# Counting a group of landed gather tiles three groups behind instead of two

## What is computed

```python
# N = 12501 nodes, D = 128, 150000 edges, LAYERS = 2
h = emb; acc = emb
for _ in range(LAYERS):
    h = segment_sum(adj_val[:, None] * h[adj_col], adj_row, num_segments=N)
    acc = acc + h
graph_item_embs = acc / (LAYERS + 1)
combined = graph_item_embs[items] + item_features[items]
...                                   # session attention, sess_emb [512, 128]
scores = (W_K * l2norm(sess_emb)) @ l2norm(graph_item_embs).T
```

## Time and profile before

| | |
|---|---|
| median of 3 runs | 4200.8 us (4196.42 to 4205.08) |
| profiled execution, its own time | 4204.8 us |
| its span, first to last instruction | 4203.0 us |
| busy: VectorE, GpSimd, TensorE, ScalarE | 3060.5, 2796.8, 2735.4, 810.9 us |
| mean granted TensorE clock | 0.771 |
| DMA moved | 231.36 MB, mean 55 GB/s |

### The profile page before, as it was taken

The page is one execution under the profiler, slowest core; times in us unless marked ns, Lnnn a source line. Parts: engine busy times, 40 slices in busy tenths (PEclk is TensorE's granted clock), DMA queues, the critical chain, the costliest instruction groups (busy, mean ns, idle before and its releaser), DMA issues.

```text
span 4203.0 us, 81683 instructions
## 1 busy us (share of the span) xinstructions
PE 2735.4 (65%) x14549; PEld 2365.5 (56%) x14550; DVE 3060.5 (73%) x7307; ACT 810.9 (19%) x2729; POOL 2796.8 (67%) x2868
## 2 busy tenths in 40 slices
PE   4999997555655566565664656565565655655798
PEld 2777776555555565555554555555555555553454
DVE  8999998867766677666665666676676766667575
ACT  0999997000000000000000000000000000004553
POOL 2477766767777777667775767677777777775770
PEclk8898898777777667777766766777777778786899
DMA  1000000222222222222225222222222222243143
GB/s 35 3 4 3 3 3 3 59 50 52 53 52 53 53 52 54 50 51 53 52 54 159 55 48 52 52 55 52 53 53 53 52 52 54 53 112 102 53 154 147
DMA packets 153059, 231.36 MB, mean 55 GB/s; under 512 B 65760, under 2 KB 106104, under 8 KB 152504
## 3 DMA queue, kind: packets, MB, share of 16 engines
q0 software_dynamic: 89760, 164.71, 16.9%
q1 hardware_dynamic: 48076, 59.06, 4.4%
q10 hardware_dynamic: 14796, 3.77, 0.7%
HBM read 186.08 MB, written 41.29 MB: 54 GB/s over the span
## 4 chain that ended last, share of the span: by engine, by line
POOL 28%; DMA 24%; issue 22%; PE 9%; DVE 9%; ACTq 4%; ACT 3%; SPq 0%; DVEq 0%; POOLq 0%
POOL ring L627 26%; DMA ring<-in_L_rec_emb,ring 12%; DMA ring<-table,ring 10%; ACTq L742 3%; PE bank L1598 2%; PE bank L1657 2%; ACT big L701 2%; DVE stage L976 1%; POOL ring L654 1%; DVE big L920 1%; PE bank L1685 1%; DVE big L936 1%; PE bank L1644 1%; POOL sorted_edges L587 1%; PE bank L1626 1%
## 5 line engine op out<-in xcount | busy, mean ns | idle before, releaser
L1598 PE MATMUL bank<-ring,shared 128*128 x9952 | 1809.1, 360 | 1248.2 <-POOLq L616 949.2
L1598 PEld LDWEIGHTS bank<-ring,shared 128*128 128x128 f32 x9952 | 1701.0, 268 | 1356.3 <-issue 1355.6
L1290 DVE TENSOR_TENSOR acc<-acc,bank 128x256 f32 x2488 | 1032.7, 415 | 945.0 <-PE bank L1598 936.8
L627 POOL DMA_INDIRECT ring<-table,ring x1146 | 1083.1, 945 | 462.4 <-issue 316.7
L627 POOL DMA_INDIRECT ring<-in_L_rec_emb,ring x1146 | 1089.0, 950 | 448.7 <-issue 318.5
L1240 DVE TENSOR_SCALAR shared<-bank,mlo,mval 128x256 f32<-128x256 f32 x2488 | 1334.9, 537 | 0.0
L717 ACT COPY mlo<-ring 128x24 f32 (+1 forms) x104 | 21.9, 211 | 2987.3 <-PE bank L1598 2372.5
L701 ACT ACTIVATE big<-big 128x68 f32<-128x68 bf16 x1764 | 557.5, 409 | 0.0
L1498 PE MATMUL bank<-big,ring 128*128 128x136 f32 x2352 | 439.8, 326 | 59.1 <-DVE ring L928 15.7
L587 POOL DMA_INDIRECT sorted_edges<-moved,block_to x313 | 400.3, 1279 | 101.5 <-issue 101.2
L1498 PEld LDWEIGHTS bank<-big,ring 128*128 128x128 f32 x2352 | 350.7, 213 | 146.4 <-ACT big L701 125.8
(11 more groups left out here) (254 smaller groups left out, 1480.5 us busy)
## 6 DMA issues: line engine op xcount, KB each, us to landing
ring<-in_L_rec_emb SPq DMA_DIRECT2D x3072, 0.5 KB
ring<-in_L_rec_emb ACTq DMA_DIRECT2D x3072, 0.5 KB
ring<-table SPq DMA_DIRECT2D x3072, 0.5 KB
ring<-table ACTq DMA_DIRECT2D x3072, 0.5 KB
scores<-stage SPq DMA_DIRECT2D x48, 512.0 KB, 2.7
ring<-in_L_rec_emb,ring POOLq DMA_INDIRECT x1146
ring<-table,ring POOLq DMA_INDIRECT x1146
table<-acc SPq DMA_DIRECT2D x7, 896.0 KB, 9.9
```

Of the source, the lines that this page charges most:

```text
L627: pool.indirect_dma_start(msg[:, j % RING, :], None, source, bass.IndirectOffsetOnAxis(m_col[:, j:j + 1], 0)).then_inc(s_g[gi % (T // GRP4 ...
L1290: add = dve.tensor_tensor(acc[:, bass.ds(off, BUCKET)], acc[:, bass.ds(off, BUCKET)], bank[u % PR][:, 0:BUCKET], ALU.add)
L1598: last = pe.matmul(bank[u % PR][:, q * D:(q + 1) * D], onehot[:, u % SR, q * P:(q + 1) * P], msg_flat[:, bass.ds(offs[u], D)], start=True, ...
```

## The change

`group_landed` is called for the group three behind the one whose gathers are about to be issued, instead of two behind; the last three groups of a layer are counted after its last gather instead of the last two. The ring keeps its 72 slots, and the gate for free slots is the same.

```diff
     RING = 3 * T
+    LATE = 3
     BEHIND = RING - (NB - 1)
...
             def gather_group(layer, source, gi):
 
-                if gi >= 2:
-                    group_landed(layer, gi - 2)
+                if gi >= LATE:
+                    group_landed(layer, gi - LATE)
                 if gi % 2 == 0 and GRP4 * gi >= RING:
                     pool.wait_ge(s_mm[M - 1], PER * layer + (GRP4 * gi + 2 * GRP4 - BEHIND) // M)
...
                     gather_group(layer, source, gi)
-                for gi in range(NGRP - 2, NGRP):
+                for gi in range(NGRP - LATE, NGRP):
                     group_landed(layer, gi)
```

## The result

The changed kernel takes 4084.4 us (median of 4 runs, 4081.2 to 4093.1), the kernel before 4201.5. The ratio is 0.9725, with a 95% interval of 0.9707 to 0.9744: 117 us, or 2.75%, faster. Forecast were 143 us and 4058 us; the time lies within the range of 4028 to 4110.

The account below looks back on a forecast made before the run. GpSimd's gathers and their waits were taken as the bound. Terms -145 - 8 + 4 + 6 = -143 us off the median 4200.8 gave 4058 us, with a range of 4028 to 4110 us.

Parts of the forecast that it names:

- The bound: Both layers: the chain goes through GpSimd's gathers and what they wait for; GpSimd sets the end of each layer.
- Landing waits, -145: GpSimd's waits for landings of earlier gathers, both layers: all go if landings take as long as before, -145 us.
- the backlog: Rival: late landings are a DMA-engine backlog that grows with the slack; 4135 us if half returns, chance 0.12.
- the forecast's own range: 4029 to 4077 us, from every unknown at its better end to its worse; chance 0.78.
- Waits without a name, -8: Unattributed waits at a group's start, within the 27 us of "issue" over 0.30 each: 0 to -27, taken as -8 us.
- Counts late for TensorE, +4: Counts on GpSimd's queue reach TensorE up to 5 us later, showing at layer ends: +4 us for both layers.
- The own tile, +6: Tile fetched by SP and ACT, early rounds: landing savings return as waits for it, 0 to 14.6, taken +6 us.
- The gate: The ring's gate at line 623, early in a layer: costs 2 us today, nothing changed for it.
- The slower rival: TensorE counts later, so the own tile's loop binds for many rounds: 4266 us with 20 of 50, chance 0.05.

## Why the prediction was right, and where not

**The bound** was right. GpSimd's gathers set the end of both layers; each us of wait taken from them came off the time (sum below against 123.6 us of span).

**Landing waits, -145: mis-sized, -108.** The step that failed is "if a landing takes as long as before, all of them go". The room did exceed every wait of the kernel before, but landings grew into it: their median is 4.7, 7.3, 11.8 and 14.9 us with two, three, four and five groups. I had named this as a rival and given it 0.12, on the ground that the DMA engines were busy a quarter of the time and that 22 gathers in a row met no wait. Neither is evidence against a queue: the share is a mean over engines and says nothing of a number of DMAs, and a stretch without GpSimd waiting is not one without late landings. What followed was the sign that I had given for the backlog: landings of over 9 us, and GpSimd still waiting for them. The waits cost 36.9 us where under 15 were forecast, the gathers of the first layer reach over 1469 us where 1465 was the most, and DMA kept 19% of the chain. The time lies between the forecast's own range, which ends at 4077 us, and the backlog's, which begins at 4090. That it is within the stated range is luck as far as this step goes: only a quarter of the term was lost, but nothing in the step said so.

**Waits without a name, -8: -9.** "issue" is 649.2 - 2104 x 0.30 = 18.0 us over its base, from 27.

**Counts late for TensorE, +4: wrong in its mechanism, about -2.** I read from the earlier trace rows that the queue holds two gathers beside the running one. Without own rows and with three groups the count of the 88th group comes here, between GpSimd's gathers:

```profile
L613 POOLq EVENT_SEMAPHORE  x1: 17/17/17, 1171.3 to 1171.3; - x1
```

```profile
1168.72 0.94 POOL L624 DMA_INDIRECT ring<-in_L_rec_emb,ring  x1 [0.30 <-issue]
...
1171.22 0.94 POOL L624 DMA_INDIRECT ring<-in_L_rec_emb,ring  x1 [0.30 <-issue]
```

The group's last gather is the one at 1168.72. Ahead of its count in the queue stand the gathers of the two groups behind it, seven in all, as one of these groups has an own tile. At 1171.22 the engine is only at the second of them, so at least five are waiting. With 96 rows and five groups there are more. This is the count of a group whose last gather starts at 1277.75, with 15 gathers of four groups ahead of the count:

```profile
L617 POOLq EVENT_SEMAPHORE  x1: 17/17/17, 1282.5 to 1282.5; - x1
```

```profile
1277.75 0.94 POOL L628 DMA_INDIRECT ring<-in_L_rec_emb,ring  x1 [0.31 <-issue]
...
1281.50 0.94 POOL L628 DMA_INDIRECT ring<-in_L_rec_emb,ring  x1 [0.30 <-issue]
```

The gather at 1281.50 is the third of the 15, so 12 are waiting. The page of the Trainium skill that I had set aside, Advanced Engine Details and Errata, section Engine Queue Depths, gives GpSimd's queue 8 instructions. The trace with three groups is in keeping with that; the one with five shows more, and the measurement decides. So with three groups a count comes as soon as the data lands: without own rows the median count is 2.55 us after the group's last gather started, and the median landing 2.51. With five groups and 96 rows the count comes at 4.7 us, 2 us after the landing, and there the queue does hold it up. What I saw in the earlier trace rows was the sequencer putting four gathers into an empty queue: from the clearing at 907.9 to the next count at 909.9 it took 2.0 us, and the two counts after the landing shown above are as far apart, at 1188.99 and 1190.99. The end of a layer came no later after its last gather: 0.5 us less passes after the first layer's, and 1.5 us less from the second layer's to the end of the span, which are the -2. At the second layer's end VectorE idles 1.80 us before its last passes, and 1.84 before the change:

```profile
3696.41 0.42 DVE L1291 TENSOR_TENSOR acc<-acc,bank 128x256 f32 x1 [1.80 <-PE bank L1599]
```

**The own tile, +6: -6.** Waits for it fell from 16.7 to 10.4 + 5.3 - 18 x 0.30 = 10.3 us. The three that cost more than issue lie in the first six rounds of a layer, early as said, but they did not take over what the landings gave up. Why they became less was not tried by itself.

**The gate:** 4.9 - 16 x 0.30, nothing, from 2 us. One small term was missing: with a median of 947 instead of 945 ns the gathers of both layers are busy 2176.8 instead of 2172.1 us by the page, +5.

Sum: -108 - 9 - 2 - 6 - 2 + 5 = -122 us, against 123.6 between the two spans.

**The slower rival** did not appear: the longest wait for an own tile, 6.7 us, lies at 907.6 us, within the first six rounds.

## What to carry to other kernels

When a wait for data is moved back, ask what the data's time of arrival depends on before booking the whole wait as gain: if it ends in a queue, it will use the room. Look beside the stream that is late for another that shares its engines, and count its DMAs rather than their bytes; here a quarter fewer small DMAs (4040 us, with a part of the rows left out) gave more than one group of extra room (4084 us), and more room (five groups, 4044 us) gave nearly as much while the output stays complete. And a busy share that is a mean over many engines cannot rule out that one of them is full.

## What was not expected of the hardware

- 128 DMAs of 512 bytes a round, 2% of the DMA engines' mean time by the view above, stretch the median landing of 64 KB gathers from 2.5 us to between 4.7 and 14.9 us, by how much room they are given. 64 bytes each do the same (4.6 us with two groups), and 64 DMAs do not (2.5 us). Of a gather's 16 packets one is held up.
- GpSimd's sequencer runs at least 12 gathers ahead of the engine (five groups, 96 rows). An increment that stands behind them on its queue is executed while they still wait.
- With five groups, where landings are latest, ACT takes 11.1 us in the median for 32 of its small DMAs, against 10.6 us with two, three and four groups. Why is not shown: with four groups landings are nearly as late.
